# A Mamba-2 layer with a routed LoRA feed-forward on one core: VectorE turns all of y and B in paired groups, and the orders of VectorE, ScalarE and GpSimd around it are written anew

## What is computed

```python
x = x + mamba(layernorm(x)) + lora_ffn(layernorm(x))

# mamba: H=64 heads of P=64, state N=128, G=8 groups of 8 heads
gate, hbc, dt = split(xn @ in_proj_w.T)
xBC = silu(causal_conv4(hbc) + conv_bias)          # x, B, C
dt = softplus(dt + dt_bias);  dA = exp(-exp(A_log) * dt)
state = state * dA + (dt * x) outer B              # scan over tokens
y = state . C + x * D
yn = y * rsqrt(mean(y*y over the group) + eps) * norm_weight * silu(gate)
out = yn @ out_proj_w.T

# lora_ffn: base projection, top-2 of 8 experts, rank 16
out = xn @ W_base.T + b_base + 2 * sum_e w[e] * (xn @ A[e].T) @ B[e].T
```

## Time and profile before

| | |
|---|---|
| median of 3 runs | 3145.75 us (3145.01 to 3145.84) |
| profiled execution | 3145.09 us, its span 3143.4 us |
| TensorE busy | 3126.1 us, 99% |
| VectorE busy | 2558.5 us, 81% |
| ScalarE busy | 1704.5 us, 54% |
| GpSimd busy | 835.5 us, 27% |
| granted TensorE clock | 1.000 |

### The profile page before, as it was taken

One profiled execution on the slowest core, in us unless ns is written; L12 is line 12 of the kernel. 1 busy time (PEld: TensorE's weight loads), 2 busy tenths in 40 slices (PEclk: granted clock), 3 DMA queues, 4 the chain that ended last, 5 costly groups with the idle time before them and its releaser, 6 DMA issues.

```text
span 3143.4 us, 55218 instructions
## 1 busy us (share of the span) xinstructions
PE 3126.1 (99%) x17660; PEld 2573.4 (82%) x17660; DVE 2558.5 (81%) x4599; ACT 1704.5 (54%) x4467; POOL 835.5 (27%) x917
## 2 busy tenths in 40 slices
PE   8999999999999999999999999999999999999999
PEld 7788888887888888888788888888878888888887
DVE  7977777785589999999648999999954988989983
ACT  5766666664265555656226555556533655565551
POOL 4444434433022222222103222222210222222220
PEclk9999999999999999999999999999999999999999
DMA  8777777777665555555566555555546555555554
GB/s 290 274 265 272 264 276 266 261 256 263 232 216 194 189 201 187 189 194 201 173 225 205 191 191 191 201 184 190 209 166 236 196 195 187 195 194 201 186 189 161
DMA packets 185668, 672.63 MB, mean 214 GB/s; under 512 B 21056, under 2 KB 22208, under 8 KB 185408
## 3 DMA queue, kind: packets, MB, share of 16 engines
q1 hardware_dynamic: 161280, 584.91, 53.3%
q10 hardware_dynamic: 24128, 84.42, 7.6%
HBM read 532.41 MB, written 136.84 MB: 213 GB/s over the span
## 4 chain that ended last, share of the span: by engine, by line
PE 95%; DVE 2%; ACT 1%; DMA 1%; issue 0%; SPq 0%; POOL 0%; ACTq 0%; DVEq 0%; POOLq 0%
PE dense L1072 21%; PE dense L1074 21%; PE dense L1073 21%; PE pX L1072 7%; PE pX L1074 7%; PE pX L1073 6%; PE pY L1187 3%; PE pD L1217 1%; PE pD L1187 1%; DVE conv_us L1497 1%; PE pCB L1163 1%; PE pU L1072 1%; PE pS L1073 1%; PE pS L1072 1%; PE pS L1074 1%; PE pU L1074 1%
## 5 line engine op out<-in xcount | busy, mean ns | idle before, releaser
L1072 PE MATMUL dense<-xn_hi,w_hl 128*128 128x512 f32 (+2 forms) x2192 | 869.7, 397 | 0.8 <-POOL w_hl L444 0.5
L1074 PE MATMUL dense<-xn_hi,w_hl 128*128 128x512 f32 (+2 forms) x2192 | 853.7, 389 | 0.0
L1073 PE MATMUL dense<-xn_lo,w_hl 128*128 128x512 f32 (+2 forms) x2192 | 852.0, 389 | 0.0
L1497 DVE SCALAR_TENSOR_TENSOR conv_us<-conv_in,const_g,conv_us 128x512 f32<-128x512 f32 x576 | 480.3, 834 | 47.0 <-ACT conv_us L694 33.2
L1074 PEld LDWEIGHTS dense<-xn_hi,w_hl 128*128 128x128 f32 (+1 forms) x2192 | 409.5, 187 | 88.9
L1072 PEld LDWEIGHTS dense<-xn_hi,w_hl 128*128 128x128 f32 (+1 forms) x2192 | 409.9, 187 | 86.0 <-issue 2.2
L1073 PEld LDWEIGHTS dense<-xn_lo,w_hl 128*128 128x128 f32 (+1 forms) x2192 | 410.3, 187 | 83.5 <-issue 1.2
L1072 PE MATMUL dense<-z_hi,w_hl 128*128 128x512 f32 x820 | 324.4, 396 | 1.6 <-DVE acc L1680 1.1
L501 POOL TENSOR_TENSOR C_lo<-BC,C_hi 128x128 fp32r<-128x128 f32 x120 | 60.0, 500 | 983.5 <-ACT S_hi L736 982.9
L1074 PE MATMUL dense<-z_hi,w_hl 128*128 128x512 f32 x820 | 319.7, 390 | 0.0
L1073 PE MATMUL dense<-z_lo,w_hl 128*128 128x512 f32 x820 | 319.1, 389 | 0.0
(11 more groups left out here) (233 smaller groups left out, 5935.3 us busy)
## 6 DMA issues: line engine op xcount, KB each, us to landing
w_hl<-w_split SPq DMA_DIRECT2D x732, 512.0 KB, 3.5
w_split<-w_hl SPq DMA_DIRECT2D x244, 512.0 KB, 3.8
cum_b<-cum_scratch ACTq DMA_DIRECT2D x128, 512.0 KB, 4.9
w_raw<-w_slots_dram SPq DMA_DIRECT2D x122, 512.0 KB, 5.4
acc<-x_tr_dram ACTq DMA_DIRECT2D x16, 512.0 KB, 6.5
out_tr_dram<-acc ACTq DMA_DIRECT2D x16, 512.0 KB, 4.7
BC<-x_tok_dram SPq DMA_DIRECT2D x6, 512.0 KB, 5.3
conv_us<-x_tok_dram SPq DMA_DIRECT2D x6, 512.0 KB, 6.2
```

The source lines that it names most:

```text
L1072: nc.tensor.matmul(out, lhs[0], rhs[0], start=start, stop=False)
L1073: nc.tensor.matmul(out, lhs[0], rhs[1], start=False, stop=False)
L1074: return nc.tensor.matmul(out, lhs[1], rhs[0], start=False, stop=stop)
L1497: nc.vector.scalar_tensor_tensor(out=conv_u[r], in0=conv_in[r][:, t:t + TB], scalar=const_g[p][:, 4 * j + t:4 * j + t + 1], in1=conv_u[r], ...
```

## The change

It has four parts, all in paired groups.

- *yn.* `chunk_3` is no longer called for chunks 2 and 3 of a paired group. `yn_rows`, `gated_pair`, `z_high_pair` and `gated_lo_pair` take the pair's first chunk as an argument and run for chunks 0 and 1 and for chunks 2 and 3. The second pair is turned late in the group, between conv taps; its z_lo stands near the head of the next group. Only chunk 3 of group 0 still goes through `chunk_3` (in group 1).
- *B.* x and B, C share one tile xBC. `x_rows` turns x and B of two chunks together (32 partitions by 320), and `B_rows` is gone. x_tm is wider by N, B_tm is gone.
- *x times dt.* `chunk_1_x` is split into `wx_product` (first, so that wx_hi may start after one product) and `dtx_product`, `chunk_1_cb` into `b_low` and `cb_masked`, and these take places of their own in VectorE's order. The order of taps, silus, additions and masks is new throughout.
- *ScalarE and GpSimd.* `chunk_1` of ScalarE is split into `b_high`, `cs_high`, `ramp_relus`, `ramp_exps` and `wx_high`; for chunk 0 the high parts of B and wx stand between the two halves of the relus. B's high part no longer waits for TensorE's B·C product. The two inverse root mean squares of a pair are one addition and one power on two columns (`inv_rms_pair`), behind both squares; for chunk 2 they stand between S_lo and wx_lo, and the decay of the state behind those.

In TensorE's order the B·C product of chunk 0 stands behind gate 2, and output unit 0 ahead of 2s and 2b of chunk 0.

```diff
                     gate_unit(g, False, 0, True)
-                    if second:
-                        chunk_3(g - 1, 2, two=True)
                     gate_unit(g, False, 1, True)
+                    gate_unit(g, False, 2, True)
+                    if not second:
+                        chunk_3(0, 3)
                     chunk_1(g, 0, p, True, True)
-                    gate_unit(g, False, 2, True)
-                    chunk_3(g - 1, 3, two=second)
                     gate_unit(g, False, 3, True)
+                    out_units(g, 0, two=True)
                     chunk_2s(g, 0)
                     chunk_2b(g, 0)
-                    out_units(g, 0, two=True)
+                    out_units(g, 1, two=True)
                     chunk_1(g, 1, p, True, True)
-                    out_units(g, 1, two=True)
...
-                            src = xT[p][32 * f:32 * f + 32, :, :].rearrange("n j (c t) -> n j c t", c=NC)
-                            dst = x_tm[32 * k:32 * k + 32, :, :].rearrange("p c (j i) -> p j c i", j=XT)
+                            src = xBC[p][32 * f:32 * f + 32, 0:XT + 1, :].rearrange("n j (c t) -> n j c t", c=NC)
+                            dst = x_tm[32 * k:32 * k + 32, :, :].rearrange("p c (j i) -> p j c i", j=XT + 1)
...
+                def inv_rms_pair(g, c):
+
+                    n = chunk(q, g, c)
+                    pool.wait_ge(sq_done, n + 2 + 1)
+                    nc.gpsimd.tensor_tensor(rstd[:, :, 0], ssq[:], eps_t[:, 0:1].broadcast_to([128, 2]), ALU.add).then_inc(rstd_done, 2)
+                    pool.wait_ge(rstd_done, n * 2 + 2)
+                    nc.gpsimd.tensor_tensor(rstd[:, :, 1], rstd[:, :, 0], eps_t[:, 1:2].broadcast_to([128, 2]), ALU.pow).then_inc(rstd_done, 2)
...
                     gate_unit(0)
...
+                    cs_high(g, p, 0)
...
+                    gate_unit(2)
+                    ramp_relus(g, 0, True, 0)
+                    if second:
+                        b_high(g, 0, True)
+                        wx_high(g, 0)
+                    ramp_relus(g, 0, True, 1)
+                    gate_unit(3)
+                    ramp_exps(g, 0, True)
```

VectorE's new order in a paired group (from the second on, not the last):

```diff
+                    x_rows(g, 0, p, 0, 1)
+                    if second:
+                        silu(g - 1, 5, p)
+                        gated_lo_pair(g - 1, 1 - p, 2)
+                        prep(g)
+                        x_rows(g, 0, p, 1, 3)
+                        gate_tile(g, 0, False)
+                        x_rows(g, 0, p, 3, 4)
+                        wx_product(g, 0)
+                        gate_tile(g, 1, False)
+                        b_low(g, 0)
...
                     gate_tile(g, 2, False)
+                    dtx_product(g, 0)
+                    cb_masked(g, 0)
+                    dve.wait_ge(acc_loaded, (q + 1) * 64)
+                    out_adds(g, 0, halves=(0,), two=True)
+                    gate_tile(g, 3, False)
                     masked(g, 0, True)
...
+                        masked(g, 2, True)
+                        y_state(g, 2, True)
+                        state(g, 2)
+                        wx_product(g, 3)
+                        b_low(g, 3)
+                        yn_rows(g, p, 0, 2, 3)
+                        y_skip(g, 2, True)
+                        dtx_product(g, 3)
+                        yn_rows(g, p, 0, 3, 4)
+                        conv_tap(g, 0, p, 0)
+                        gated_pair(g, p, 0)
...
+                        y_intra(g, 2, True)
+                        y_intra(g, 3, True)
+                        conv_tap(g, 3, p, 0)
+                        conv_tap(g, 3, p, 1)
+                        conv_tap(g, 3, p, 2)
+                        silu(g, 2, 1 - p)
+                        yn_rows(g, p, 2, 0, 2)
+                        silu(g, 3, 1 - p)
+                        conv_tap(g, 4, p, 0)
+                        yn_rows(g, p, 2, 2, 3)
+                        conv_tap(g, 4, p, 1)
+                        yn_rows(g, p, 2, 3, 4)
+                        conv_tap(g, 4, p, 2)
+                        conv_tap(g, 5, p, 0)
+                        gated_pair(g, p, 2)
+                        conv_tap(g, 5, p, 1)
+                        silu(g, 4, 1 - p)
+                        conv_tap(g, 5, p, 2)
```

More of the change, by code:

```diff
@@ L719, in load_cum, with b_high @@
                                   .broadcast_to([128, HPG, Q])).then_inc(cumb_loaded[c % 2], 16)
+                def b_high(g, c, two=False):
+                    n = chunk(q, g, c)
+                    if two:
+                        act.wait_ge(xt_done, xt_n(q, g, c))
+                        act.wait_ge(st_done, upd_n(q, g, c, last_block) - 1)
+                    else:
+                        act.wait_ge(s1, n * 2 + 2)
+                    nc.scalar.activation(B_hi[:], x_tm[:, c % 2, GC:GC + N] if two else pCB[:, 0:N], ACT.Copy).then_inc(ck_evac, 1)
@@ L723, in wx_high @@
                     nc.scalar.activation(wx_hi[:], wx[:], ACT.Copy).then_inc(wx_hi_done, 1)
[L725 to L745, removed]
@@ L746, in chunk_1, with ramp_relus @@
+                def ramp_relus(g, c, two, half):
+                    E_c = E_2[half_of(two, c)]
+                    if half == 0:
+                        if c == 0:
+                            act.wait_ge(prep_done, q * PREPS + g + 2)
+                        act.wait_ge(cumb_loaded[c % 2], (q * (2 * G) + g * 2 + (c // 2 + 1)) * 16)
+                    for h in range(4 * half, 4 * half + 4):
                         ins = nc.scalar.activation(E_c[:, h, :], cum_b[c % 2][:, h, :], ACT.Relu, scale=-1.0,
@@ L753, in chunk_1, with ramps, next_cum @@
                                              scale=-1.0).then_inc(exp_done, 1)
[L754 to L759, removed]
+                def ramps(g, c, two=False):
+                    ramp_relus(g, c, two, 0)
+                    ramp_relus(g, c, two, 1)
+                    ramp_exps(g, c, two)
+                def next_cum(g, c, last):
                     if c < 2:
@@ L1217, in chunk_3 @@
                         mm = nc.tensor.transpose(pD0[:, j * 128:(j + 1) * 128], yn[c % 2][:, j * 128:(j + 1) * 128], ident[:])
-                    mm.then_inc(s3, 3 if two and c == 2 else 1)
+                    mm.then_inc(s3, 1)
                 def dt_slot(first_tile, end_tile):
@@ L1366, in paired_group @@
                     chunk_2y(g, 3, True)
-                    x_units(2)
-                    if last:
-                        chunk_3(7, 2, two=True)
-                        x_units(1)
-                        chunk_3(7, 3, two=True)
-                        x_units(1)
+                    x_units(4 if last else 2)
                 group(0, 0, first=True)
@@ L1560, in chunk_1_cb @@
                     nc.vector.tensor_tensor(CBm, pCB[:, N:N + Q], causal[:], ALU.mult).then_inc(cbm_done, 1)
[L1561 to L1562 removed]
+                    nc.vector.tensor_tensor(B_lo[:], pCB[:, 0:N], B_hi[:].bitcast(F32), ALU.subtract).then_inc(bl_done, 1)
                 def skip(g, c):
@@ L1648, in gated_lo, with yn_rows @@
                         .then_inc(z_done, 1)
-                def yn_rows(g, p, first, end):
+                def yn_rows(g, p, c, first, end):
                     if first == 0:
-                        dve.wait_ge(yn_done, chunk(q, g, 1) + 1 + 1)
+                        dve.wait_ge(yn_done, chunk(q, g, c) + 2 + 1)
                     for f in range(first, end):
```

369 lines of the change are left out of this document (211 added, 158 removed).

## The result

The changed kernel takes 3129.14 us (median of 5 runs, 3125.92 to 3132.66) against 3145.01 us in the same session (5 runs, 3143.97 to 3145.84). The ratio is 0.9949, with a 95% interval of 0.9935 to 0.9964: 15.9 us or 0.5% faster. The forecast was 3126.5 us with a range of 3123 to 3143. The runs of the changed kernel lie 6.7 us apart, those of before 1.9 (15 later runs of the kernel before lie 3.9 us apart).

The account below looks back on a forecast made before the run. TensorE's instruction stream was taken to bound the paired groups, with VectorE at 92%. Taking 20.0 us of transposes off the median 3145.75 gave 3125.8 us; with 0.7 for block-edge waits, 3126.5 us, range 3123 to 3143.

Parts of the forecast that it names:

- TensorE's loss: 168 yn transposes leave TensorE: 0.49 and 0.46 us in each of 21 paired groups, 20.0 us in all.
- VectorE's needs: VectorE's work in a paired group: 82.9 us without contention, plus 2.0 contention and 3.1 waits, 88.0 against 87.13.
- the drift d: How far VectorE falls behind TensorE per paired group: taken as 0.2 us, with an error of about 1.
- a walk: VectorE's new order followed step by step, contention partly falling into waits: it closes at 0 to 0.3 us a group.
- The list of contention: Places in a paired group where VectorE's instructions meet GpSimd's: 2.0 us in sum, bounds 0 and 4.0.
- rival 2: VectorE becomes the bound in paired groups, contention staying at 4.0 us: d of 2.5, 3164 us; chance 0.13.
- The tightest: Smallest room for VectorE's lateness: chunk 1's masked E, wanted at 41.4 us and ready at 39.1, margin 2.3 us.
- the formula 3 x (6d - 2.3): Cost of drift d over three blocks with six group-to-group steps each: nothing at 0.2, the whole gain at 1.5.
- signs of being right: 176 yn transposes on TensorE, paired groups of 87.1 us, VectorE about 85 busy, x_tm transposes near 503 ns.
- signs of being wrong: TensorE waiting for masked E or an addition, growing groups, VectorE over 86 us, B_lo, y_skip or gate tiles over 1.
- rival 1: VectorE drifts 0.7 to 1.2 us a paired group, giving back 5.7 to 14.7: 3131 to 3141 us; chance 0.22.
- Rivals 3 and 4: Rival 3: a new wait at each block's end, 3138 us, chance 0.05; rival 4: transposes were hidden, 3146 us, chance 0.04.

Follow-up runs that it names:

- the first and the last mended kernel: The changed kernel with x times dt of chunk 0 behind its masks, 3125.65 us; with x times dt of chunks 0 and 3 moved, 3125.11 us.

## Why the prediction was right, and where it was not

*TensorE's loss was right to the hundredth.* 87.12 us against 87.13, and with VectorE's lateness taken away the time is 3125.1 to 3125.7 us against the 3125.8 of the sum. The idle transposes brought the old time back, but for 0.09 us a group.

*VectorE's needs were nearly right in sum.* x_tm transposes 502 ns against 503; waits for ScalarE 2.8 us with small gaps against 3.1. Contention was put at 2.0 us and is 2.6 in most groups of blocks 1 and 2, worked out as the sum of the parts over each instruction's least length, and 3.7 in some.

*The step that was mis-sized is the drift d,* taken as 0.2 us a group. The masks of chunk 3 fall back by 0.45 to 0.5 us a group, and once TensorE waits for VectorE a group takes VectorE's own time, 87.6 us: d = 0.5. In a group with the second hit it is 88.7, so d = 1.6. The sum of needs had 0.9 as the most; the lower figure came from a walk that assumed contention to fall into waits. The list of contention put the collision with chunk 0's wx_lo on gate tile 2, at up to 1.0 us, and chunk 3's on y plus skip, at 0.6. It left out the x products, although rival 2 names them and the rule of the Trainium skill that stands beside it (SBUF — State Buffer, SBUF: two separate sides) covers every VectorE instruction with two SBUF inputs beside a GpSimd instruction that reads SBUF; the trace agrees with it, 1.78 us against 0.68. Gate tile 2 got off free because it started first, and the product behind it paid 1.10. In chunk 3 the product paid 0.85, and y plus skip 0.90 more now and then. With the first of these products out of the way, the drift is the 0.2 of the forecast.

*The places were weighed wrongly.* The tightest was said to be chunk 1's mask with 2.3 us of room, and chunk 3's had 3.7. In the trace TensorE reaches chunk 1's mask 42.4 us after a group's start and not 41.4, since the matmuls of chunk 0 come first; VectorE, where it is not late, has that mask's first half ready by 38.4, so some 4 us fit in. Chunk 3's mask starts at 71.5 where VectorE is not late; at 74.0 TensorE loses nothing and at 74.5 it loses 0.3, so between 2.5 and 3.0 us fit in. The silu of C, where TensorE stops under more load, is not in the working.

*So the 2.6 us by which the median missed the forecast are not the drift alone.* A drift of 0.5 adds up to 3 us over a block's six steps, about what chunk 3's mask has room for; alone it would cost about 0.1 us a block, by the estimate above. The 4.5 us of blocks 1 and 2 are the four second hits of this execution, which the working has nowhere. Where the time falls within some microseconds of the forecast hangs on their number, and that it fell as near as it did is luck in that sense; the median is 0.1 us over the forecast's own narrow range of 3124 to 3129. Block 3 lost nothing, which the formula 3 x (6d - 2.3) overlooked.

*Its own signs are mixed.* Of the signs of being right, 176 transposes are left on TensorE and x_tm's take 502 ns. VectorE's busy time is 82.5 to 83.0 us, not 85; the 85 did not follow from the prediction's own sum, 82.9 + 2.0 with 1.9 us of gaps in it. Of the signs of being wrong, three came: waits for a mask, groups that grow from 87.1 to 87.6 and 88.7 us, and y plus skip over 1 us. They are the signs of rival 1.

*Rival 1* (a little drift) is what happened in kind, at the weaker end: 3129 where it began at 3131. *Rival 2* was right that VectorE stands at the edge; 1 us more at the head of each group cost 10 of the 15.9 us. *Rivals 3 and 4* did not come about. From its first B·C product the last group of block 3 runs to the end in 119.7 us instead of 126.6; 5.4 of the difference is that this product now stands one gate unit later, and the other 1.4 is what the transposes behind it had cost (0.46 + 0.95), with nothing lost at the tail. And the transposes had not been hidden.

*One reading of the kernel before was mistaken.* The prediction took VectorE's 5.2 us of waits as time that it could partly give up. They were not slack: 1 us at the head of a group cost 19 us, the same microsecond inside one of the waits nothing.

What stays open is why the hundredths fall as they do in one group and not in another; no run was made for it. That the second hit makes the runs of the changed kernel spread by 6.7 us is argued from its 1.15 us and from the 2.5 and 2.9 us spreads of the first and the last mended kernel, not shown by a trace of each run; 15 runs of the kernel before spread by 3.9.

## What to carry to other kernels

When one engine is busy all the time, price work taken off it by the distance of neighbouring starts; that came within 0.1 us a group here. Then ask of the engine that takes the work over not how idle it is but where: only a wait for the bounding engine is slack for lateness, while a wait for a chain that it started itself is room for work at that very place. To find which kind there is, put a small idle load at two places and compare.

Where two engines lock each other out, look at the instruction behind the one that overlaps, and fill the time of the lock with instructions that do not take part in it.

## What the hardware showed that was not expected

VectorE instructions with two SBUF inputs that begin while GpSimd works on a 128x512 or 128x128 tile stand still until it ends: 1.78 us instead of 0.68 for a 128x512 product beside a wx_lo of 1.81. In the changed kernel's trace such a 128x512 instruction that began 0.02 us or more behind GpSimd's ended 0.55 us behind it, whenever it had begun, in all of 147 cases. If VectorE begins 0.02 us earlier, it takes 0.68 and GpSimd's instruction grows to 1.81 instead of 1.29. Beside GpSimd's root mean square instructions (128x1 and 128x2) the silus and conv taps were not slowed (by 0.01 us at most). Nor were the 32x256 and 32x320 transposes and the instructions that read PSUM (by 0.02 us at most). Of the instructions with one SBUF input at least one was: const_g, 0.42 us instead of 0.18.
